# Maxima turned in another bank, first units ahead of the last normed block, and a shorter routing in a six-layer decoder

## The chip, the cores and the metric

The kernel runs on one core of a Trainium2 chip. The metric is device time in microseconds (us) of one execution. The engines named are PE (TensorE, matrix products and transposes), DVE (VectorE), ACT (ScalarE), POOL (GpSimd), and SP (SyncE, which here only issues DMAs). They run side by side, each its own queue in order, and meet at semaphores.

## The reference

Sixteen sequences of 128 tokens with 256 features go through six residual blocks. `_layernorm` is a plain normalisation; each block adds its result to `x`:

```
x = x + _L0_attn_ref(_layernorm(x), ...)      # causal bucket attention, LN, MLP with GELU (256 -> 1024 -> 256)
x = x + _L0_xattn_ref(_layernorm(x), ctx, ...)  # cross attention, rotary with decay
x = x + _L0_ffn_ref(_layernorm(x), ...)       # RMS norm, attention, then a routed MLP:
    topw, topi = top_k(softmax(h2 @ router_w), 2); topw = softmax(topw)      # 8 experts of 512
    moe_out = swiglu(h2, shared) + sum over the 2 experts of topw * swiglu(h2, expert)
x = x + _L1_attn_ref(_layernorm(x), ...)      # retention: (Q K^T * decay) V, group norm
x = x + _L1_xattn_ref(_layernorm(x), ctx, ...)  # cross attention, window of 64, causal
x = x + _L1_ffn_ref(_layernorm(x), ...)       # 16 experts of 128 in 4 groups: the 2 best groups,
    # in them the 2 best experts by softmax score + gate_b; weights from the plain softmax; a shared expert
```

## The kernel before

The program names the stages ATT0, MLP, XATT0, ATT1, MOE0, RET, XATT1 and MOE1. A tile (`Tile`: layer `l`, number `t`) is one sequence of 128 tokens; `x_all` holds all sixteen in on-chip memory. Five hand-written programs, one for each engine, give the order; every hand-over is a semaphore that counts up, `wait(eng, name, tile)`.

`pipeline(eng, layers, step)` runs the attention layers. A step holds several tiles at different ages: `at[3]` is normalised (`variance`, POOL's `inverse_root`, `normalise`, PE's transpose at L979), `at[2]` rotated, `at[1]` gets its values and maxima, `at[0]` its scores and probabilities, `at[-1]` its output product L1044 and the residual addition L1864, and `normed(at)`, which is `at[-2]` where a feed-forward layer follows, is normalised for that layer (L1893, L1895), transposed by PE (`turn_normed`, L1088) and copied and split by ACT and POOL into `fT_hi` and `fT_lo`. In the same late steps POOL splits the coming layer's first weights in pieces (`first_low`, L850).

The row maxima go this way: DVE reduces the scores (L1734), works them in several small operations into `nmx` (L1749 to L1762), PE transposes it (`turn_maxima`, L1052) into PSUM bank `B_V`, which also holds the values and at times the output product, and DVE spreads it into `inj` (`inject`, L1777), which PE adds to the scores by a product.

The dense feed-forward parts (`feed_forward`, MLP and the shared expert of MOE0) take four groups of four tiles (`GT` = 4, `GROUPS` = 4). `up` (L1159) makes, for each unit `fc` of 128 hidden features, 6 matmuls of 512 columns for MLP and 12 for MOE0 (gate and up), as each operand is split in a high and a low part and three products are made. The two units' banks alternate: unit `fc` waits for `act_done` of unit `fc - 2`. `down` (L1159 too) gives `down_out`, `add` (L2198) sums into `x_all` and gives `acc_done`.

The routed parts gather rows. DVE finds each token's two experts (`gate_moe0`, `gate_moe1`), `place` makes running counts over the sixteen tiles by four additions of shifted copies (L2022), PE's `ranks` turn them into ranks, and `slots(f, k)`, k = 0 to 5, make each token's slot; two tables of ones and zeroes (`slot_tile`, `slot_row`, L2071 and L2030) and PE's `origins` (L1221) give for every slot its row (`from_u`). Then tiles of 128 slots (39 in MOE0, 47 in MOE1) run one after another: POOL gathers rows (L684), PE transposes (L1277) and multiplies (L1292, L1304) with the tile's own expert weights, which SP loads (`load_tiles`, L567) into 4 buffers of 1.5 MB (MOE0) or 8 of 385 KB. In MOE0 tile 0 has its buffer early; tiles 1 to 3 wait for the last `acc_done`:

```
sp.wait_ge(S["acc_done"], units("acc_done", f, F_EXPERTS[f] - 1, GROUPS - 1, GT))
```

In MOE0 the steps of the routing (`gate_moe0(0 .. 15)`) are laid between the hidden units of the shared expert; number 15 is `slots(MOE0, 5)`, which waits for PE's `origins` (`hot_out`). In MOE1 all lies between the last attention step and the first tile. MOE0's results come back through DRAM into `y_back` and are added to `x_all` by `combine` (L2289, L2290), tile by tile in RET's first steps. `gate_piece(at)` says which piece of MOE1's gating belongs to a step of XATT1.

## Time and profile before

| | |
|---|---|
| median of 3 runs | 1462.07 us (1457.41 to 1466.78) |
| the profiled execution | 1464.77 us, its span 1462.9 us |
| mean granted TensorE clock | 0.953 of full speed |
| PE busy | 1298.5 us, 89% |
| DVE, ACT, POOL busy | 867.4, 571.1, 705.6 us |
| chain that ended last | PE 61%, DVE 14%, DMA 10%, POOL 5% |

The span runs from the first to the last instruction of one execution. Busy shares are means over stages of different kinds; the chain says which engine's work set the end. The granted clock is in parts of the full 2.4 GHz; 0.50 in a stretch is 1.2 GHz. In the rows below, L and a number is the line of the kernel, and the square bracket is the idle time of that engine ahead of the instruction, with what ended it.

### The profile page before, as it was taken

To read this page: it belongs to the slowest core of one execution; us is meant where nothing else is said; L and a number is where in the kernel's file an instruction comes from. 1 tells how busy PE (TensorE), PEld (TensorE's weight loads), DVE (VectorE), ACT (ScalarE), POOL (GpSimd) and SP (SyncE) were. 2 spreads that over 40 slices of the span, in tenths; PEclk is the share of its full clock that TensorE was granted. 3 is DMA by queue.
4 is the path that set the end of the run, shared out by engine and by line. 5 is a ranking of instruction groups with operands and counts; after the bars stand their busy time and mean duration, and the time that the engine had idled before them with its cause. 6 is when DMAs were issued, how large, how long until landed. Compare 5 with 4: busy or idle time off the path is not lost.

```text
span 1462.9 us, 33803 instructions
## 1 busy us (share of the span) xinstructions
PE 1298.5 (89%) x12132; PEld 1045.0 (71%) x12132; DVE 867.4 (59%) x2050; ACT 571.1 (39%) x1272; POOL 705.6 (48%) x949
## 2 busy tenths in 40 slices
PE   5999979988999999979889999959998999818897
PEld 4666647876777777758889999846765777617776
DVE  4888743337888888736512121158875778773346
ACT  2555535523444455643222222214443555413331
POOL 5566632017667466630223333237784556427426
PEclk9999968998999999989999999979999999958999
DMA  6000000020000000000298999630000000028964
GB/s 252 2 2 0 2 1 30 1 86 16 13 15 5 2 16 15 16 16 1 80 338 314 334 325 328 245 137 30 0 16 9 25 28 26 16 92 284 316 189 144
DMA packets 47370, 137.79 MB, mean 94 GB/s; under 512 B 6925, under 2 KB 29646, under 8 KB 41104
## 3 DMA queue, kind: packets, MB, share of 16 engines
q1 hardware_dynamic: 32944, 110.37, 21.4%
q0 software_dynamic: 7536, 19.67, 4.4%
q10 hardware_dynamic: 6768, 6.16, 1.2%
q8 instruction: 70, 1.15, 0.3%
q14 instruction: 52, 0.43, 0.1%
HBM read 119.54 MB, written 17.56 MB: 94 GB/s over the span
## 4 chain that ended last, share of the span: by engine, by line
PE 61%; DVE 14%; DMA 10%; issue 8%; POOL 5%; ACT 1%; DVEq 0%; SPq 0%; POOLq 0%; ACTq 0%
PE ps L1159 11%; PE ps L1018 8%; PE ps L967 7%; PE ps L1292 7%; PE ps L1066 5%; DMA back_of<-w_odd 4%; DMA row_in<-rows_of,from_u 4%; PE ps L1304 3%; PE ps L1035 3%; PE ps L1044 3%; DVE negmax L1734 3%; PE ps L911 2%; PE ps L958 2%; PE ps L1073 2%; PE ps L993 2%
## 5 line engine op out<-in xcount | busy, mean ns | idle before, releaser
L1292 PE MATMUL ps<-hT,w_tile 128*128 128x128 f32 x1624 | 199.9, 278 | 8.4 <-DMA w_tile<-in_w_f 7.4
L1292 PEld LDWEIGHTS ps<-hT,w_tile 128*128 128x128 f32 x1624 | 190.6, 194 | 12.6 <-issue 7.1
L1358 ACT ACTIVATE probsT_all<-ps 128x1024 f32<-128x1024 f32 x128 | 131.1, 1024 | 158.3 <-PE ps L967 158.3
L1734 DVE TENSOR_REDUCE negmax<-ps 128x8 f32<-128x1024 f32 x128 | 155.9, 1218 | 54.2 <-PE ps L967 53.9
L967 PE MATMUL ps<-qe,kf 32*128 32x256 f32 x1280 | 152.9, 386 | 0.0
L967 PE MATMUL ps<-ke,qf 32*128 32x256 f32 x1024 | 143.6, 398 | 0.0
L747 POOL TENSOR_SCALAR eps_sum<-mv 128x1 f32<-128x1 f32 x112 | 25.4, 227 | 201.0 <-DVE mv L1671 169.4
L967 PEld LDWEIGHTS ps<-qe,kf 32*128 32x128 f32 x1280 | 110.4, 189 | 4.9 <-issue 2.7
L2255 DVE TENSOR_TENSOR h_in<-ps,act_sb 128x512 f32<-128x512 f32 x39 | 27.0, 691 | 143.3 <-PE ps L1292 143.3
L1066 PE MATMUL ps<-probsT_all,va 128*32 128x128 f32 x2560 | 104.4, 281 | 6.1 <-ACT probsT_all L1358 4.4
L691 POOL DMA_INDIRECT back_of<-be,to_u x39 | 39.4, 1010 | 144.7 <-DVE be L2268 144.7
L1304 PE MATMUL ps<-w_tile,h_in 128*128 128x256 f32 x406 | 102.6, 382 | 4.0 <-DVE w_odd L2268 4.0
L1351 ACT ACTIVATE hT<-ps,vecs 128x128 f32<-128x128 f32 x142 | 47.0, 384 | 151.3 <-PE ps L1277 136.8
L1018 PE MATMUL ps<-hT,w_even 128*128 128x128 f32 x640 | 90.3, 288 | 9.2 <-issue 4.7
L1066 PEld LDWEIGHTS ps<-probsT_all,va 128*32 128x32 f32 x2560 | 62.3, 110 | 50.6 <-issue 29.3
L1018 PEld LDWEIGHTS ps<-hT,w_even 128*128 128x128 f32 x640 | 80.6, 198 | 20.3 <-issue 13.3
L967 PEld LDWEIGHTS ps<-ke,qf 32*128 32x128 f32 x1024 | 90.6, 186 | 3.2 <-issue 0.8
L1350 ACT ACTIVATE hT<-ps 128x256 f32<-128x256 f32 x95 | 36.3, 382 | 129.3 <-PE ps L979 61.0
L684 POOL DMA_INDIRECT row_in<-rows_of,from_u x63 | 61.1, 970 | 45.2 <-issue 19.6
L1304 PEld LDWEIGHTS ps<-w_tile,h_in 128*128 128x128 f32 x406 | 70.9, 191 | 11.2 <-issue 4.1
L837 POOL TENSOR_TENSOR fT_lo<-act_sb,fT_hi 128x256 fp32r<-128x256 f32 (+1 forms) x48 | 34.9, 727 | 87.0 <-ACT fT_hi L1350 84.3
L766 POOL TENSOR_TENSOR ke<-kf,const 128x512 f32<-128x512 f32 x64 | 67.2, 1050 | 19.3 <-ACT kf L1351 17.8
(266 smaller groups left out, 3226.8 us busy)
## 6 DMA issues: line engine op xcount, KB each, us to landing
w_tile<-in_w_f SPq DMA_DIRECT2D x39, 1536.0 KB, 9.3
w_tile<-in_w_f SPq DMA_DIRECT2D x47, 385.0 KB, 7.3
back_of<-w_odd ACTq DMA_DIRECT2D x47, 128.0 KB
ctxT<-in_ctxT SPq DMA_DIRECT2D x32, 128.0 KB, 2.1
rows_of<-nv SPq DMA_DIRECT2D x32, 128.0 KB, 1.7
w_even<-in_w_att SPq DMA_DIRECT2D x3, 1024.0 KB, 7.2
y_back<-back_of SPq DMA_DIRECT2D x6, 512.0 KB, 5.0
x_all<-in_x SPq DMA_DIRECT2D x4, 512.0 KB, 10.6
```

Of the source, the lines that this page charges most:

```text
L684: nc.gpsimd.indirect_dma_start(row_at(b), None, rows_dram[f], bass.IndirectOffsetOnAxis(ap=from_u[:, j:j + 1], axis=0)).then_inc(S["row_in ...
L766: return nc.gpsimd.tensor_tensor(dst, src.unsqueeze(2).to_broadcast([P, KC, 2, P]), parity.unsqueeze(1).unsqueeze(3).to_broadcast([P, KC, ...
L967: done[name, half] = mm(ps[:, bank, c * D:(c + 1) * D], a[strip(j), c], b[strip(j), c].rearrange("p i k -> p (i k)"), start=first, stop=fi ...
L1018: last = mm(ps[:, B_QK, m * P:(m + 1) * P], w[:, c, m * P:(m + 1) * P], src[:, c, :], start=(c == 0), stop=(c == KC - 1))
L1035: last = mm(ps[:, B_V, 0:D], src[:, c, :], w[:, c, 2 * D:3 * D], start=(c == 0), stop=(c == KC - 1))
L1066: last = mm(ps[VW * (h % HB):VW * (h % HB + 1), B_O, h // HB * P:(h // HB + 1) * P], va[:, tile.p, h, :], probsT_all[:, (j * HB + n) * P:( ...
L1159: ins = mm(out, a, b, start=first and k == 0, stop=last and k == 2)
L1292: last = mm(ps[:, 2 * which + at.two, fc * P:(fc + 1) * P], w[:, col:col + P], rowT[:, at.two, c, :], start=c == 0, stop=c == KC - 1)
L1304: last = mm(ps[:, 4 + at.two, 0:D], h_in[:, at.two, fc * P:(fc + 1) * P], w[:, first + fc * D:first + (fc + 1) * D], start=fc == 0, stop=f ...
L1351: return nc.scalar.activation(dst, src, ACT.Identity, scale=1.0 if scale is None else scale, bias=0.0 if bias is None else bias)
L1358: nc.scalar.activation(half_of(probsT_all, half), ps[:, 2:4].rearrange("p b n -> p (b n)"), ACT.Exp, scale=HD ** -0.5).then_inc(S["probs"], 1)
L1734: nc.vector.tensor_reduce(m, ps[:, 0:2].rearrange("p b (h k) -> p (b h) k", h=HB), AX.X, ALU.max, negate=True).then_inc(S["s_max"], 1)
```

## The change

1. `turn_maxima` writes bank 2, `inject` reads it there. It waits for the maxima and for the previous tile's probabilities (the reader of bank 2) in place of the values and the residual.
2. POOL does `first_low` ahead of `norm_low`.
3. PE does the first units of the coming dense layer (`FIRST_UNITS`: MLP 2, MOE0 1) ahead of the last normed block's transposes.
4. XATT0's first norm: DVE's `variance` stands ahead of the last group's additions of MLP, POOL's root ahead of its wait for them.
5. MOE0's step 15 of the routing goes behind the additions of the third group. Tile 1's buffer is `w_back`, the memory of `y_back`; its load waits for the last `h_done`, those of tiles 2 and 3 for the last `down_out`.
6. RET's first tiles (`rooted`): the combination stands behind the norm for tile 0, and tile 2's variance, combination and norm go into the step of tile 1.
7. MOE1's routing: one gating piece moves up a step; `place` goes, PE counts straight from `chosen` (`late_ranks`); `slot_row` is built in 32 comparisons with one column of `part` each (`part` is f32 now); the table is scaled by steps of 128 rows so that one accumulation gives the row (`late_origins`), POOL scales the last 8 of 32 blocks; `slots(MOE1, 5)` is one operation.

```diff
+FIRST_UNITS = {MLP: 2, MOE0: 1, MOE1: 0}
+LATE_BLOCKS = 24
-            return (w_tile0, w_tile1, w_tile2, w_tile3)[b][:, 0:f_cols(f)]
+            return (w_tile0, w_back, w_tile2, w_tile3)[b][:, 0:f_cols(f)]
...
+                    elif j == 1:
+                        sp.wait_ge(S["h_done"], units("h_done", f, F_EXPERTS[f] - 1, GROUPS - 1, D_CHUNKS[f]))
                     else:
-                        sp.wait_ge(S["acc_done"], units("acc_done", f, F_EXPERTS[f] - 1, GROUPS - 1, GT))
+                        sp.wait_ge(S["down_out"], units("down_out", f, F_EXPERTS[f] - 1, GROUPS - 1, GT))
...
+                first_low(at)
                 norm_low(normed(at))
-                first_low(at)
...
             def turn_maxima(tile):
                 wait(pe, "nm_sb", tile)
-                wait(pe, "va_sb", tile)
-                out = tile.back(2)
-                wait(pe, "x_done", tile.back(3) if out is not None and out.l == RET else out)
-                tr(ps[:, B_V, 0:P], nmx[:], ident).then_inc(S["m_out"], 1)
+                wait(pe, "probs", tile.back(1))
+                tr(ps[:, 2, 0:P], nmx[:], ident).then_inc(S["m_out"], 1)
...
+                first_units(normed(at))
                 turn_normed(normed(at), at)
...
+                first = rooted(at)
+                if first and not first_crossed(first[0]):
+                    variance(first[0])
...
+                for tile in first[1:]:
+                    variance(tile)
+                    combine(MOE0, tile.t + 1)
+                    normalise(tile)
...
+            def hot_rows(f, k):
+                if f == MOE1:
+                    for i in range(k * NT, (k + 1) * NT):
+                        last = ts(slot_row[:, i], iota_all[:], part[:, 1, i:i + 1], None, ALU.is_equal)
...
+                if step_ == 4 and f == MOE1:
+                    dve.wait_ge(S["tile_nth"], 2)
+                    for a, b, last in ((0, NT, NT), (NT, LATE_BLOCKS, LATE_BLOCKS - NT)):
+                        table = slot_tile[:, a:b, 0:m]
+                        tt(table, table, steps_of[:, 0:last].unsqueeze(2).to_broadcast([P, last, m]), ALU.mult).then_inc(S["row_hot"], 1)
+                    hot_rows(f, 1)
...
+                    if f == MOE1:
+                        ts(from_u[:, 0:m], ps[:, 0, 0:m], -1.0, 0.0, ALU.add, ALU.max).then_inc(S["from_done"], 1)
+                        return
...
-                        if f == MOE0:
+                        if f == MOE0 and fc + 1 < n or f == MOE0 and g + 1 < GROUPS:
                             gate_moe0(q)
...
+                            if f == MOE0 and g + 1 == GROUPS:
+                                gate_moe0(GROUPS * n - 1)
...
+                if f == MLP:
+                    dve.wait_ge(S["acc_done"], units("acc_done", f, n_e, 0, GT))
+                    variance(tiles_of(XATT0, 0))
                 add(n_e, n_e % 2, GROUPS - 1)
```

**PE, from the last attention step of ATT0 into MLP.** Here is PE's order before; L1044 is the last output product, L1088 a normed block's transposes, L1159 MLP's first products.

```order
L993 MATMUL ps<-const,o 128x128 x2
L1088 MATMUL ps<-const,nv 128x128 x2
L1044 MATMUL ps<-w_even,oT 128x256 x2
L1088 MATMUL ps<-const,nv 128x128 x2
L1159 MATMUL ps<-fT_hi,w_hi 128x512
L1159 MATMUL ps<-fT_lo,w_hi 128x512
L1159 MATMUL ps<-fT_hi,w_lo 128x512
L1159 MATMUL ps<-fT_hi,w_hi 128x512
L1159 MATMUL ps<-fT_lo,w_hi 128x512
```

And in the changed kernel, where L1056, L1098 and L1114 are the same three:

```order
L1056 MATMUL ps<-w_even,oT 128x256 x2
L1114 MATMUL ps<-fT_hi,w_hi 128x512
L1114 MATMUL ps<-fT_lo,w_hi 128x512
L1114 MATMUL ps<-fT_hi,w_lo 128x512
L1114 MATMUL ps<-fT_hi,w_hi 128x512
```

(the next eight rows are L1114 too, then)

```order
L1098 MATMUL ps<-const,nv 128x128 x2
L1114 MATMUL ps<-fT_hi,w_hi 128x512
L1114 MATMUL ps<-fT_lo,w_hi 128x512
L1114 MATMUL ps<-fT_hi,w_lo 128x512
L1114 MATMUL ps<-fT_hi,w_hi 128x512
```

Two units, twelve products in all, now stand between the last output product and the last normed block.

**DVE, end of MOE0's shared expert.** Before; L2085 to L2094 are the eight operations of the routing's last step, L2198 the additions, L2255 the first tile's.

```order
L2185 TENSOR_TENSOR hid_lo<-h_tmp,hid_hi 128x512
L2085 COPY scratch<-ps 128x39
L2086 TENSOR_SCALAR scratch<-ps 128x39
L2087 TENSOR_TENSOR scratch<-scratch,ps 128x39
L2088 SCALAR_TENSOR_TENSOR scratch<-scratch 128x39
L2089 TENSOR_SCALAR from_u<-scratch 128x39
L2091 TENSOR_SCALAR scratch<-scratch 128x39
L2092 SCALAR_TENSOR_TENSOR scratch<-ps,scratch 128x39
L2094 SCALAR_TENSOR_TENSOR to_u<-scratch 128x39
L2198 TENSOR_TENSOR x_all<-ps,x_all 128x256 x8
L2255 TENSOR_TENSOR h_in<-ps,act_sb 128x512 x2
```

And in the changed kernel, L2181 to L2189 and L2293:

```order
L2280 TENSOR_TENSOR hid_lo<-h_tmp,hid_hi 128x512
L2293 TENSOR_TENSOR x_all<-ps,x_all 128x256 x4
L2181 COPY scratch<-ps 128x39
L2182 TENSOR_SCALAR scratch<-ps 128x39
L2183 TENSOR_TENSOR scratch<-scratch,ps 128x39
L2184 SCALAR_TENSOR_TENSOR scratch<-scratch 128x39
L2185 TENSOR_SCALAR from_u<-scratch 128x39
L2186 TENSOR_SCALAR scratch<-scratch 128x39
L2187 SCALAR_TENSOR_TENSOR scratch<-ps,scratch 128x39
L2189 SCALAR_TENSOR_TENSOR to_u<-scratch 128x39
L2293 TENSOR_TENSOR x_all<-ps,x_all 128x256 x4
L2354 TENSOR_TENSOR h_in<-ps,act_sb 128x512 x2
```

The routing's eight operations moved from ahead of eight additions to between two groups of four.

**DVE, the second half of MOE1's routing.** Before, from the casts of the slots on (L2062):

```order
L2062 CAST part<-part_u 128x64
L2065 TENSOR_SCALAR scratch<-ends,nth 47x16
L2066 TENSOR_REDUCE expert_f<-scratch 47x1
L2067 TENSOR_SCALAR expert_of<-expert_f 47x1
L2071 TENSOR_TENSOR slot_tile<-iota_all,part 128x1504
L2030 TENSOR_TENSOR slot_row<-iota_all,part 128x2048 x2
L2078 TENSOR_TENSOR slot_tile<-slot_tile,iota_all 128x752
L2085 COPY scratch<-ps 128x47
L2086 TENSOR_SCALAR scratch<-ps 128x47
L2087 TENSOR_TENSOR scratch<-scratch,ps 128x47
L2088 SCALAR_TENSOR_TENSOR scratch<-scratch 128x47
L2089 TENSOR_SCALAR from_u<-scratch 128x47
```

And in the changed kernel:

```order
L2149 CAST part<-part_u 128x64
L2152 TENSOR_SCALAR scratch<-ends,nth 47x16
L2153 TENSOR_REDUCE expert_f<-scratch 47x1
L2154 TENSOR_SCALAR expert_of<-expert_f 47x1
L2158 TENSOR_TENSOR slot_tile<-iota_all,part 128x1504
L2103 TENSOR_SCALAR slot_row<-iota_all,part 128x128 x16
L2165 TENSOR_TENSOR slot_tile<-slot_tile,steps_of 128x752
L2165 TENSOR_TENSOR slot_tile<-slot_tile,steps_of 128x376
L2103 TENSOR_SCALAR slot_row<-iota_all,part 128x128 x16
L2176 TENSOR_SCALAR from_u<-ps 128x47
```

Two wide comparisons are 32 narrow ones, one table operation is two, and five operations at the end are one.

## Rows read from the trace of the kernel before

**Rows 1.** Page, part 4: chain of work that ended last, share of the span by engine
```profile
PE 61%; DVE 14%; DMA 10%; issue 8%; POOL 5%; ACT 1%; DVEq 0%; SPq 0%; POOLq 0%; ACTq 0%
```

**Rows 2.** Timeline, XATT0: start us, us, engine, line, op, out<-in, count, [idle before <-releaser]
```profile
396.36 0.41 DVE L1864 TENSOR_TENSOR x_all<-ps,x_all 128x256 f32 x1
...
396.91 0.30 PE L1052 MATMUL ps<-const,nmx 128*128 128x128 f32 x1 [0.29 <-DVE x_all L1864]
```

**Rows 3.** Waits: who waits <- for what: us, waits, longest
```profile
PE ps L1052 <- DVE x_all L1864: 5.1, 13, 1.1
```

**Rows 4.** Timeline, a steady step of ATT0, DVE
```profile
129.90 0.18 DVE L1671 BATCH_NORM_AGGREGATE mv<-stats 128x2 f32<-128x6 f32 x1
130.01 0.69 DVE L1777 TENSOR_TENSOR inj<-ps,const 128x512 bf16<-128x512 f32 x1
```

**Rows 5.** Timeline, a late step of ATT0, where the first weights are split
```profile
183.52 0.17 DVE L1749 TENSOR_SCALAR nmx<-negmax 128x16 uint32<-128x16 uint32 x1
...
184.32 1.27 POOL L850 TENSOR_TENSOR w_lo<-w_first,w_hi 128x514 fp32r<-128x514 f32 x1
...
184.43 1.19 DVE L1749 TENSOR_SCALAR nmx<-nmx 128x16 uint32<-128x16 uint32 x1
...
186.31 0.30 PE L1052 MATMUL ps<-const,nmx 128*128 128x128 f32 x1 [2.48 <-DVE r_all L1864]
```

**Rows 6.** Windows: us, PE PEld DVE ACT POOL busy, PEclk, DMA, GB/s
```profile
188.00:192.00 4.00, 4.00 (x27) 2.80 (x24) 2.08 (x4) 1.26 (x2) 1.53 (x3) 0.50 0.00 0
```

**Rows 7.** Timeline, end of ATT0 and start of MLP
```profile
222.60 0.69 PE L1088 MATMUL ps<-const,nv 128*128 128x128 f32 x2 [2.88 <-DVE nv L1895]
...
226.00 0.67 ACT L1569 ACTIVATE h_tmp<-ps,f_bias 128x512 f32<-128x512 f32 x1
...
228.20 0.46 PE L1159 MATMUL ps<-fT_hi,w_hi 128*128 128x512 f32 x1
```

**Rows 8.** Timeline, first step of XATT0
```profile
318.19 0.66 PE L979 MATMUL ps<-const,u 128*128 128x128 f32 x2 [3.10 <-DVE u L1700]
```

**Rows 9.** Timeline, last normed block ahead of MOE0
```profile
646.75 0.69 PE L1088 MATMUL ps<-const,nv 128*128 128x128 f32 x2 [2.33 <-DVE nv L1893]
```

**Rows 10.** Timeline, end of MOE0's shared expert and its first tiles
```profile
719.26 0.36 PE L1159 MATMUL ps<-w_hi,hid_hi 128*128 128x256 f32 x1 [2.18 <-DVE x_all L2198]
...
727.91 2.56 SPq L567 DMA_DIRECT2D w_tile<-in_w_f  x3
...
734.83 2.39 PE L1292 MATMUL ps<-hT,w_tile 128*128 128x128 f32 x19 [2.30 <-DMA w_tile<-in_w_f]
```

**Rows 11.** Timeline, RET's first steps
```profile
976.37 0.69 PE L979 MATMUL ps<-const,u 128*128 128x128 f32 x2 [3.15 <-DVE u L1700]
```

**Rows 12.** Timeline, routing of MOE1
```profile
1282.99 0.38 DVE L2008 TENSOR_TENSOR hot<-const,idx_f 128x16 f32<-128x16 f32 x2
...
1284.51 0.41 DVE L1999 MAX8 top<-sc 128x8 f32<-128x16 f32 x4
...
1294.67 0.22 DVE L2156 TENSOR_TENSOR chosen<-hot,sc 128x64 bf16<-128x64 f32 x1
...
1297.46 0.42 DVE L2044 TENSOR_TENSOR scratch<-n_all,steps_of 128x256 f32<-128x256 f32 x1
...
1299.21 0.42 DVE L2052 SCALAR_TENSOR_TENSOR scratch<-ends,scratch 128x256 f32<-128x256 f32 x1
...
1304.28 4.48 DVE L2030 TENSOR_TENSOR slot_row<-iota_all,part 128x2048 bf16<-128x2048 bf16 x2
...
1308.68 0.93 DVE L2078 TENSOR_TENSOR slot_tile<-slot_tile,iota_all 128x752 bf16<-128x752 bf16 x1
...
1310.97 1.46 PE L1221 MATMUL ps<-slot_tile,slot_row 128*128 128x47 bf16 x32 [0.52 <-POOL slot_tile L698]
...
1313.43 0.19 DVE L2089 TENSOR_SCALAR from_u<-scratch 128x47 uint32<-128x47 f32 x1
```

**Rows 13.** Groups by line and form, a tensor_scalar: busy us, mean ns
```profile
L1893 DVE TENSOR_SCALAR nv<-r_all,rstd 128x256 f32 x8 | 2.8, 348 | 0.0
```

More of the change, by code:

```diff
@@ L1027, in project_values @@
                 wait(pe, "va_sb", last)
-                if last is not None and last.l != RET and tile.l != RET:
-                    wait(pe, "inj_sb", last)
                 if tile.l == RET and isinstance(tile.t, int) and tile.t == 0:
@@ L1896, in norm_rows, with rooted @@
                 ins.then_inc(S["n_norm"], 1)
+            def rooted(at):
+                if 3 not in at or at[3].l == RET and at[3].t == 2:
+                    return []
+                tile = at[3]
+                return [tile, tiles_of(RET, 2)] if tile.l == RET and tile.t == 1 else [tile]
             def combine_next(at):
```

185 lines of the change are left out of this document (120 added, 65 removed).

## The prediction, made before the changed kernel ran

> **What bounds the kernel now.** I read the page first: the chain that ended last lies on TensorE (PE) for 61% of the span, on VectorE (DVE) for 14% and on DMA for 10% [rows 1]. An edit therefore pays only where PE stands still, or where the joints between layers run through DVE, ScalarE (ACT) and GpSimd (POOL) one after another. So I took the list of waits for the instructions that the diff touches, then the timeline around each, and asked of every wait which of its inputs came last.
>
> The own time of the profiled execution is 1464.8 us (span 1462.9 and about 2 around it); the three runs shown have a median of 1462.1, so it stands 2.7 above that median. The sum is made against 1464.8. About 1% (14.7 us) is what a measurement of this kernel can tell from no change.
>
> **1. Maxima into bank 2: 4.0.** Before, the transpose of the maxima (L1052) writes the bank of the values and so waits for the residual addition L1864 that reads it; after, it writes bank 2 and needs only `nmx` and the previous tile's probabilities, which PE has used already. At 396 us `nmx` is done by about 396.4, the addition starts 396.36, and PE goes on at 396.91 after 0.29 idle that the addition ended [rows 2]. All such waits for `x_all` come to 5.1 us in 13 cases [rows 3]; where `nmx` itself is as late, nothing comes back, so I take 4.0 (bounds 3 and 5.1). For ATT0 the steady steps give nothing: the injection L1777 that the transpose feeds stands behind an aggregate on DVE's own queue, 129.90 and then 130.01 [rows 4].
>
> **2. POOL's order at the tails: 2.2, and 2.9 for the clock.** Before, the split of the coming layer's first weights (`first_low`, L850) runs after `norm_low` and falls beside DVE's L1749: that bitwise operation starts 0.11 after POOL's 1.27 and takes 1.19, where another of it takes 0.17, and PE's next transpose has stood still for 2.48 [rows 5]. In each of the two last full steps of ATT0 about 1.0 comes back, and about 0.35 by part 1, as there the transpose also waited for `r_all`: 2.7. At ATT1 the same exchange puts a 768-column piece (about 1.27 x 768/514 = 1.9 us) ahead of the norm's work: it may now hold DVE's L1749 for up to 2 (I take 1.5), while in the drain the norm's root no longer stands behind it (about 1.0). Net 2.7 - 1.5 + 1.0 = 2.2. The clock: behind the 2.48 pause the granted clock fell to 0.50 (1.2 GHz) for all of 188 to 192 [rows 6]; that alone costs 2.0, and with the ends of the stretch I estimate 2.9. With a pause of 1.2 instead I let it stay up (upper bound 2.9, lower 0).
>
> **3. Two units of MLP ahead of the last normed block: -2.0.** Before, PE idles 2.88 until 222.60, turns the last block and then works at half speed, 0.63 a matmul, until 228.20 [rows 7]. The two units' 12 matmuls are those of that stretch, 5.2 us; put into the pause at the same clock they end some 2 after the block is ready. What PE fills, others lose: ACT copies the transposed block, loads a table and only then does the first Gelu at 226.00 [rows 7], and all of it stands behind the block's transposes, which now come 1.0 to 1.5 later; the two units' results sit waiting, and the third needs the bank that the first Gelu frees: it starts at 227.7 to 228.5, as before, after a pause of some 3.5 that keeps the clock down for another such stretch. I take -2.0 (bounds +0.5 and -3).
>
> **4. First cross norm ahead of the sums: 2.7.** Before, the last MLP addition is followed by statistics, POOL's root, `u`, and PE's transpose at 318.19 after 3.10 idle [rows 8]. Moved ahead of the four last additions, this chain lies under the last down products; what stays is one addition, its semaphore, and DVE's `u`. I put the transpose near 316.2: 2.0. A pause of 1.1 instead of 3.1 may keep the clock: 0.7 more as a mean over that.
>
> **5. One unit of MOE0 ahead of its last norm: 2.5.** PE idles 2.33 until 646.75 [rows 9]; the first unit stands behind that block. One unit goes into that pause and past it; a second unit has the other banks and waits for nobody. The pause is 2.3; the wait for the block's copy, which is filled too, adds something, and the lateness that the unit gives to the block takes some: 2.5, bounds 1.5 and 3.
>
> **6. Tail of MOE0: 5.8.** Three things. `gate_moe0(15)`, which waits for the origin counts, goes behind the additions of the third group, so PE no longer idles 2.18 at 719.26. Tile 1's weights now lie in `y_back`, which is free until the results are fetched back behind the last tile, so their load waits for `h_done` and not for the last sum; it was issued at 727.91 and PE waited 2.30 for it until 734.83 [rows 10]. Tiles 2 and 3 wait for `down_out`. With a load of 6.9 us (727.91 to 734.83) issued ahead of the last down products, well over 7 earlier, tile 1 is no longer late; tile 0 is bounded by its gathered rows. 2.18 + 2.30 + about 1.3 of a clock that falls less: 5.8 (bounds 4 and 7; the loads and the gathers now share the DMA engines, up to 1.5).
>
> **7. RET's joint: 1.2.** PE idles 3.15 at 976.37 for tile 2's `u` [rows 11], because two combinations stand ahead of it on DVE. They move a step earlier, but the shuffle and the rotation of the tile before bound the step nearly as much: 1.2 (0.9 to 5.0, the latter if PE becomes the bound).
>
> **8. Routing of MOE1: 4.7.** It lies wholly on the path: tiles can't start before `from_u`. (a) One piece of the group before the last moves to an earlier step: L2008 at 1282.99 to the maxima at 1284.51 are 1.5 us. (b) Between `chosen` (ends 1294.89) and the position L2052 (1299.21) lay 4.3 us: four scans, PE, two copies, then the ends. Now PE counts straight from `chosen` (0.5), and compare, reduce and four additions remain, 1297.46 to 1299.21, 1.75 [rows 12]: 2.1 saved. (c) From 1304.28 to the end of `from_u` at 1313.62 lie 9.34: two comparisons in 4.48, 0.93 of table, PE's last 32 products in 1.46 and five small operations. After: 16 small comparisons, table 0.93 + 0.5, 16 again, 32 products, one operation [rows 12]. The price of one 128x128 `tensor_scalar` isn't in the trace. Below: 0.10, one of the four maxima that take 0.41 together at 1284.51. Above: 0.348, which L1893 takes for 256 columns [rows 13]. Nearest is an operation of half those columns with overlapping ends, 0.15: then 2.4 + 1.4 + 2.4 + 1.5 + 0.4 = 8.1, 1.2 saved. At 0.10 it is 2.8 saved, at 0.348 5.1 lost. 1.5 + 2.1 + 1.2 = 4.8; 4.7, since POOL's share of the table (376 instead of 752 columns) must end before the last 16 products and may be held up by DVE.
>
> Two comparisons of 2048 columns of bf16 took 4.48 us, 0.9 columns a ns [rows 12]. The Trainium skill ("VectorE: DVE Perf Modes", the table of tiers) gives a `tensor_tensor` in bf16 twice that rate (1.22 us for 2048), and a `tensor_scalar` in bf16 four times; the trace disagrees on the first, where an operand is broadcast. By its second figure, 128 columns would be 0.03 plus what is fixed, and part 8 an estimated 1.6 more than I take. Its section "The TRN2 errata — SBUF-src ops pay a fixed extra latency per instruction" speaks against cutting one operation into 16; by it the split gives nothing or loses; no row here has such small comparisons.
>
> **Sum.** 4.0 + 2.2 + 2.9 - 2.0 + 2.7 + 2.5 + 5.8 + 1.2 + 4.7 = 24.0. 1464.8 - 24.0 = 1440.8; the same off the median would be 1438.1. I say 1440.
>
> **Rivals.**
> (A) Half is swallowed: what PE gains ahead of a stage is given back inside it, since the tile stages follow their weight loads, the clock falls anyway at two of the three places (-4.6 for parts 2 and 4), and part 6 gives only the 2.18. Then 24.0 - 4.6 - 3.6 - 1.5 = 14.3: 1450. For it speaks that part 3 loses by this very mechanism, against it that the pauses [rows 5, 8, 10] have named releasers that the diff removes.
> (B) The ceiling: all upper bounds of 2, 6 and 7, and 0.10 in part 8: 24 + 1.2 + 3.8 + 1.6 + 2.5 (part 3 neutral) = 33, so 1432.
> (C) The change doesn't do what it says at the joints, because a new wait takes the old one's place in each of parts 3 to 7 (the injection, the rotation, the gather are all within 1 us of what is removed): only parts 1 and 8 and 2.0 remain, 11: 1454.
> (D) Slower: the 32 small comparisons. At 0.348 part 8 gives 3.65 - 5.1 = -1.4 alone. For the whole to be slower than before they must cost 24 us more than forecast, 0.9 each, about what an operation costs when DVE and POOL hold each other back as in [rows 5]: there L1749 took 1.0 more than usual. POOL's table lies beside only some of them, so this needs a price that nothing here shows. From 0.45 each on the gain is under 1%. Time at 1.0 each: 1440.8 + 32 x 0.85 = 1468.
>
> **How the numbers follow.** The forecast 0.50 (1434 to 1446), A 0.22, B 0.10, C 0.14, D 0.04. Each term errs on its own by 1 to 3 us and the runs shown differ by 9, which gives every case a width of about 5 to either side. The range 1427 to 1455 holds most of the first four: below it half of B's tail, above it half of C and D. The bound of faster by over 1% is 1447.4: the forecast nearly whole, B, and 0.3 of A and a little of C: 0.73. Slower by over 1% needs 1476.7: 0.02. The rest, 0.25, is within 1%.
>
> **What would show it.** Right: PE's transpose of the maxima without a wait for `x_all`; L1749 at 0.2 to 0.4 in ATT0's tail and a granted clock near 1.0 behind it; PE's pause ahead of the first cross norm near 1; no wait of tile 1 for its weights; `from_u` ending 8 after the first row comparison begins and the small comparisons near 0.15 each. Wrong: comparisons over 0.25 each, the clock down at the same places, the third unit of MLP well before 227 (then part 3 is a gain), or tiles of MOE0 slowed by gathers. My estimate rests most on part 6 and on the clock of part 2.

## The result, and the profile of the changed kernel

| | before | changed |
|---|---|---|
| median of 3 runs | 1462.07 (1457.41 to 1466.78) | 1446.43 (1442.32 to 1447.47) |
| ratio | | 0.9868 (0.983 to 0.9907) |
| profiled execution | 1464.77, span 1462.9 | 1447.47, span 1445.6 |
| mean granted clock | 0.953 | 0.961 |

The change is faster by 1.3%. The chain that ended last, part 4 of its page, now lies on PE for more of the span, and on DVE, DMA and POOL for less [rows 1]:

```profile
PE 70%; DVE 12%; DMA 8%; issue 5%; POOL 3%; ACT 2%; DVEq 0%; SPq 0%; POOLq 0%; ACTq 0%
```

Where the time went is read best from marks that both programs have: the starts of PE's transposes of the maxima (64 of them), the DVE operations on the hidden units, on the routing and on the tiles. Each cell is the length from the mark before, in us; every mark is the start of its instruction, and the last one is the last residual addition, 2.7 before the end of the span:

| from the mark before to | before | changed | won | forecast (part) |
|---|---|---|---|---|
| ATT0, 2nd maxima (from the start) | 39.01 | 44.18 | -5.17 | |
| ATT0, 13th maxima | 123.57 | 123.26 | 0.31 | 0 (1) |
| MLP, 9th hidden unit | 82.63 | 77.31 | 5.32 | 2.7 + 2.9 (2), -2.0 (3) |
| MLP, last hidden unit | 60.11 | 60.38 | -0.27 | 0 |
| XATT0, 1st maxima | 34.72 | 31.02 | 3.70 | 2.7 (4) |
| XATT0, 15th | 133.75 | 130.44 | 3.31 | 4.0 (1) |
| ATT1, 13th | 129.56 | 129.69 | -0.13 | 0 |
| ATT1, 16th | 26.02 | 26.93 | -0.91 | -1.5 (2) |
| MOE0, 9th hidden unit | 56.04 | 57.06 | -1.02 | 1.0 (2), 2.5 (5) |
| MOE0, last hidden unit | 27.35 | 27.35 | 0 | 0 |
| 2nd tile's `h_in` | 25.95 | 19.54 | 6.41 | 5.8 (6) |
| last tile's | 212.11 | 211.40 | 0.71 | 0 |
| XATT1, 1st maxima | 159.51 | 159.20 | 0.31 | 1.2 (7) |
| XATT1, 16th | 156.81 | 156.57 | 0.24 | 0 |
| MOE1, last `chosen` | 27.53 | 25.25 | 2.28 | 1.5 (8a) |
| `slot_row` | 9.61 | 7.40 | 2.21 | 2.1 (8b) |
| last operation of the routing, `from_u` | 9.15 | 8.74 | 0.41 | 1.2 (8c) |
| tiles and residual additions, to the last addition | 146.80 | 147.09 | -0.29 | 0 |

All that lies behind the start won 22.5 together. The start took 5.2 longer in this execution; that is no doing of the change, as the first run below shows. Each column is one execution, and some of the stages below differ by more than the change between executions of the same instructions.

The rows that answer to those shown of before are these. The timeline of XATT0, beside [rows 2]: the transpose starts 0.17 after the addition has begun and waits for nothing; of the waits of [rows 3] none is left.

```profile
392.18 0.41 DVE L1921 TENSOR_TENSOR x_all<-ps,x_all 128x256 f32 x1
...
392.35 0.29 PE L1062 MATMUL ps<-const,nmx 128*128 128x128 f32 x1
```

The end of ATT0, beside [rows 5]: POOL's split now lies ahead of the bitwise operation L1806, which takes 0.17, and PE's pause is 1.04 instead of 2.48. The two windows (columns as in [rows 6]) show the clock at full speed, the first one there, the second behind the joint of MLP and XATT0.

```profile
185.67 1.27 POOL L862 TENSOR_TENSOR w_lo<-w_first,w_hi 128x514 fp32r<-128x514 f32 x1
...
189.41 0.17 DVE L1806 TENSOR_SCALAR nmx<-nmx 128x16 uint32<-128x16 uint32 x1
...
189.85 0.33 PE L1062 MATMUL ps<-const,nmx 128*128 128x128 f32 x1 [1.04 <-DVE negmax L1816]
```

```profile
188.00:192.00 4.00, 2.04 (x30) 1.16 (x29) 3.59 (x13) 1.75 (x5) 1.41 (x3) 1.00 0.00 0
318.00:322.00 4.00, 2.71 (x24) 2.47 (x24) 0.92 (x3) 1.42 (x5) 0.61 (x1) 1.00 0.95 338
```

Into MLP, beside [rows 7]. Times in the two traces are best counted from the start of the last output product, which is the first row here for the kernel before and the second for the changed one:

```profile
217.64 2.07 PE L1044 MATMUL ps<-w_even,oT 128*128 128x256 f32 x4
```

```profile
216.66 2.07 PE L1056 MATMUL ps<-w_even,oT 128*128 128x256 f32 x4
...
218.17 0.99 PE L1114 MATMUL ps<-fT_hi,w_hi 128*128 128x512 f32 x1
...
220.54 0.40 PE L1114 MATMUL ps<-fT_hi,w_lo 128*128 128x512 f32 x1
...
221.15 0.41 DVE L1952 TENSOR_SCALAR nv<-r_all,mv,rstd 128x256 f32<-128x256 f32 x1 [1.05 <-POOL rstd L826]
...
221.94 0.40 PE L1114 MATMUL ps<-fT_hi,w_lo 128*128 128x512 f32 x1
...
222.18 0.38 PE L1098 MATMUL ps<-const,nv 128*128 128x128 f32 x2
...
225.28 0.67 ACT L1626 ACTIVATE h_tmp<-ps,f_bias 128x512 f32<-128x512 f32 x1
...
226.09 0.47 PE L1114 MATMUL ps<-fT_hi,w_hi 128*128 128x512 f32 x1 [3.53 <-ACT h_tmp L1626]
```

The early products begin at 218.17 and are at full speed by 220.54; the last of the twelve starts at 221.94. The last block, ready at 221.56, is turned at 222.18: 5.5 behind the output product, where it was 5.0 before. The third unit waits 3.53 for the first Gelu and starts 9.4 behind the output product, where it was 10.6.

Then XATT0's first transpose, beside [rows 8]: a pause of 1.17 for 3.10.

```profile
316.27 0.41 PE L993 MATMUL ps<-const,u 128*128 128x128 f32 x2 [1.17 <-DVE u L1757]
```

MOE0's first tiles, beside [rows 10]: tile 1's products (weights in `y_back`) follow tile 0's without a pause.

```profile
718.22 0.44 PE L1334 MATMUL ps<-const,row_in 128*128 128x128 f32 x2 [0.52 <-DVE x_all L2293]
...
719.52 3.81 PE L1349 MATMUL ps<-hT,w_tile 128*128 128x128 f32 x32 [0.17 <-ACT hT L1408]
...
723.39 3.74 PE L1349 MATMUL ps<-hT,y_back 128*128 128x128 f32 x32
```

RET's first steps, beside [rows 11], on PE and DVE: new pauses of 2.50 and 1.89 stand in place of the 3.15.

```profile
963.26 2.69 PE L1032 MATMUL ps<-hT,w_odd 128*128 128x128 f32 x16 [2.50 <-ACT hT L1407]
...
969.56 2.34 DVE L1784 TENSOR_TENSOR probsT_all<-ps,const 128x1024 f32<-128x1024 f32 x2
...
970.92 0.75 PE L1076 MATMUL ps<-probsT_all,va 128*32 128x128 f32 x16 [1.89 <-DVE probsT_all L1784]
```

MOE1's routing, beside [rows 12]; in brackets again the idle time ahead and what ended it:

```profile
1279.58 0.22 DVE L2251 TENSOR_TENSOR chosen<-hot,sc 128x64 bf16<-128x64 f32 x1
...
1281.93 0.42 DVE L2134 SCALAR_TENSOR_TENSOR scratch<-ends,ps 128x256 f32<-128x256 f32 x1
...
1286.98 3.27 DVE L2103 TENSOR_SCALAR slot_row<-iota_all,part 128x128 bf16<-128x128 bf16 x16
...
1288.72 0.83 POOL L710 TENSOR_TENSOR slot_tile<-slot_tile,steps_of 128x376 bf16<-128x376 bf16 x1 [14.64 <-ACT tile_in L1408]
...
1295.72 0.21 DVE L2176 TENSOR_SCALAR from_u<-ps 128x47 uint32<-128x47 f32 x1 [1.55 <-PE ps L1252]
...
1296.79 1.16 POOL L693 DMA_INDIRECT row_in<-rows_of,from_u  x1 [7.24 <-DVE from_u L2176]
...
1300.29 0.69 PE L1334 MATMUL ps<-const,row_in 128*128 128x128 f32 x2 [4.60 <-DMA row_in<-rows_of,from_u]
```

### The profile page after: what moved, and what is told of

Read it like the earlier page. It is cut to its first block, busy times and chain, and to the rows that moved or that the text cites. A ratio compares the mean times of both kernels' runs of the same rounds, so it can differ in the third digit from the quotient of the medians.

```text
span 1445.6 us, 33878 instructions
## 1 busy us (share of the span) xinstructions
PE 1301.3 (90%) x12165; PEld 1048.3 (73%) x12165; DVE 863.6 (60%) x2071; ACT 571.2 (40%) x1272; POOL 702.4 (49%) x949
## 4 chain that ended last, share of the span: by engine, by line
PE 70%; DVE 12%; DMA 8%; issue 5%; POOL 3%; ACT 2%; DVEq 0%; SPq 0%; POOLq 0%; ACTq 0%
PE ps L1114 11%; PE ps L981 9%; PE ps L1032 9%; PE ps L1349 8%; PE ps L1076 6%; PE ps L1056 4%; PE ps L1047 4%; PE ps L1361 4%; DMA row_in<-rows_of,from_u 4%; DMA back_of<-w_odd 3%; PE ps L925 2%; PE ps L972 2%; DVE negmax L1791 2%; PE ps L1083 2%; PE ps L1007 2%
## 5 line engine op out<-in xcount | busy, mean ns | idle before, releaser
L1349 PE MATMUL ps<-hT,w_tile 128*128 128x128 f32 x1304 | 161.9, 278 | 0.6 <-ACT act_sb L1673 0.2
L1349 PEld LDWEIGHTS ps<-hT,w_tile 128*128 128x128 f32 x1304 | 153.3, 193 | 3.1 <-issue 0.8
L1076 PEld LDWEIGHTS ps<-probsT_all,va 128*32 128x32 f32 x2560 | 62.8, 110 | 51.8 <-issue 30.4
L1032 PEld LDWEIGHTS ps<-hT,w_even 128*128 128x128 f32 x640 | 83.0, 203 | 20.4 <-issue 13.2
L1361 PE MATMUL ps<-w_tile,h_in 128*128 128x256 f32 x326 | 83.8, 383 | 9.5 <-DVE w_odd L2367 9.4
L2280 DVE TENSOR_TENSOR hid_lo<-h_tmp,hid_hi 128x512 fp32r<-128x512 f32 x56 | 38.8, 693 | 54.8 <-ACT hid_hi L1407 54.8
```

The costliest lines, as they stand in the source:

```text
L1032: last = mm(ps[:, B_QK, m * P:(m + 1) * P], w[:, c, m * P:(m + 1) * P], src[:, c, :], start=(c == 0), stop=(c == KC - 1))
L1076: last = mm(ps[VW * (h % HB):VW * (h % HB + 1), B_O, h // HB * P:(h // HB + 1) * P], va[:, tile.p, h, :], probsT_all[:, (j * HB + n) * P:( ...
L1349: last = mm(ps[:, 2 * which + at.two, fc * P:(fc + 1) * P], w[:, col:col + P], rowT[:, at.two, c, :], start=c == 0, stop=c == KC - 1)
L1361: last = mm(ps[:, 4 + at.two, 0:D], h_in[:, at.two, fc * P:(fc + 1) * P], w[:, first + fc * D:first + (fc + 1) * D], start=fc == 0, stop=f ...
```

## The experiments

Each run changes one thing in the changed kernel, where nothing else is said. In two of the four groups of runs every kernel takes longer in the last stage (64 us for 51), and the kernel before is slower there by as much (medians of 1482 and 1484 for 1464 and 1465), so times are compared as ratios to the kernel before on the same chip, or as stages between the marks above.

**The changed kernel once more.** No edit.

> The changed kernel itself once more, to see what repeats. Theory A (the stages of the first trace are the change's doing): the start up to the third tile's transposes, the half-speed stretches of TensorE at the end of ATT0 (from about 202), at the end of ATT1 (from about 627) and the stage lengths repeat within 0.5 us; ratio 0.983 to 0.991. Theory B (the 4.7 us longer start, and the clock that fell at 627 instead of 641, are chance of one execution): at least one of them differs in this trace, by 2 us or more.

Median 1465.11, before 1482.22; ratio 0.9864 (0.9836 to 0.9892). The start up to the second maxima took 39.11, not 44.18, and 38.3 to 39.9 in each of the eleven other runs below: the 5.2 are chance. Less this shift the clock fell where it had in the first trace (at 198 and 621, there at 203 and 627), and the stages up to MOE0's tiles repeat within 0.5. Behind them two do not: MOE0's tiles took 2.1 more, and the way to the last `chosen` 30.27 instead of 25.25. So theory B holds for the start and for these two, and theory A for the stages between, as far as two executions tell.

MOE0's tiles, from the second to the last, took from 205.6 to 214.5 us in all the fourteen traces, and the edits below don't order them. The clock is not the reason, being at full speed almost throughout; PE waits for gathered rows. Here are these waits in the shortest (`first_low` first at ATT0 only, 205.6) and in the repeated changed kernel (213.5), as us in total, times, longest:

```profile
PE ps L1338 <- DMA row_in<-rows_of,from_u: 1.0, 1, 1.0
```

```profile
PE ps L1334 <- DMA row_in<-rows_of,from_u: 7.3, 9, 1.6
```

What makes the gathers late in one execution and not in another stays open.

**POOL's order.**

```diff
-                first_low(at)
                 norm_low(normed(at))
+                first_low(at)
```

> The changed kernel with one edit undone: POOL does norm_low ahead of first_low again. Theory A (the order of POOL brought the gain at the end of ATT0 and cost something at the end of ATT1): at the end of ATT0 DVE's L1806 beside the split takes 1.2 again instead of 0.2, the pause of PE is about 2.1 (2.5 less the 0.35 of the bank), the clock falls near 186 to 190, and 3 to 5 us are lost there; at the end of ATT1 0.5 to 0.9 come back and the clock falls near 641 and not near 627, 2.5 more; total +0 to +2 us. Theory B (the bank alone keeps the clock up at ATT0's end): the clock stays up to 200 there, only 1 to 2 us are lost, and the total is 1 to 2 us faster than the changed kernel.

Ratio 0.9831 (0.9806 to 0.9857). DVE's L1806 was blocked again, with PE's pause at 2.06:

```profile
184.54 1.27 POOL L862 TENSOR_TENSOR w_lo<-w_first,w_hi 128x514 fp32r<-128x514 f32 x1
...
184.65 1.19 DVE L1806 TENSOR_SCALAR nmx<-nmx 128x16 uint32<-128x16 uint32 x1
...
186.10 0.33 PE L1062 MATMUL ps<-const,nmx 128*128 128x128 f32 x1 [2.06 <-DVE negmax L1816]
```

From the 13th maxima of ATT0 to MLP's ninth hidden unit 80.87: 3.6 of the 5.3 won there are lost without the order (1.02 in the first of the two steps, the rest in the second and in the clock, which fell near 188 again). At the end of ATT1 1.06 came back (9.32 and 8.11 for 9.84 and 8.65). Theory A, but for the clock at ATT1's end: it fell at 625, not near 641. The time of the whole doesn't show the 3.6: the median is 1459.03 against 1465.11 of the changed kernel on the same chip, lower and not higher, with intervals of the ratios that overlap.

**The order at ATT0's end alone.** `first_low` first only where `normed(at)` is ATT0's.

> The changed kernel, but first_low ahead of norm_low only where MLP follows (end of ATT0); ahead of MOE0 norm_low comes first again. Theory A (at ATT1's end the early split delays DVE and POOL, PE gets more pauses and its clock falls 14 us earlier): the step at 606 loses nothing (0.6 to 0.9 back) and the clock stays up until about 640: 2.5 more, so 3 to 3.5 us faster than the changed kernel. Theory B (the earlier fall of the clock is chance or comes from elsewhere): only 0.6 to 0.9 us back and the clock falls near 627 all the same.

Ratio 0.9827 (0.9801 to 0.9853). The 1.06 came back. From ATT1's last maxima to MOE0's ninth hidden unit it took 53.02 instead of 57.03, the clock being down only from 630 to 633. By itself this speaks for theory A; the next paragraph shows that it doesn't settle it.

**What the clock does by itself.** The same stretch, from ATT1's last maxima to MOE0's ninth hidden unit, in the eight executions that have the changed kernel's instructions up to there: six from 56.98 to 57.52, but also 52.30 and 50.70. The length goes with the time for which the clock was down between the two marks: 17 us in the six, 3.4 us in the one of 52.30, none in the one of 50.70. With POOL's other order it is 56.04 (before) and 55.91 with 13.7 us, 53.02 and 52.97 with 3.4 us. At the end of XATT1 the way to the last `chosen` took 25.1 to 25.3 in eight of the thirteen traces of the changed kernel and its variants, 26.4 in three and 30.3 to 30.4 in two, with edits that don't touch it. Two executions, both with the same instructions up to here, in windows of 4 us (columns as in [rows 6]); first the repeated changed kernel, where the clock falls in the first window and stays down, then the run called `gate_moe0` back below, where it doesn't fall at all:

```profile
618.00:622.00 4.00, 2.31 (x17) 1.48 (x17) 2.22 (x6) 2.30 (x4) 2.35 (x5) 0.88 0.10 33
622.00:626.00 4.00, 3.99 (x29) 2.37 (x29) 0.00 (x0) 0.77 (x3) 0.96 (x1) 0.50 0.00 0
```

```profile
618.00:622.00 4.00, 2.46 (x24) 1.68 (x28) 2.02 (x6) 2.24 (x4) 2.47 (x4) 1.00 0.09 33
622.00:626.00 4.00, 3.99 (x52) 2.81 (x44) 0.72 (x2) 2.13 (x5) 1.18 (x2) 1.00 0.00 0
```

A fall there costs up to 6.8 us, more than any row of the table above won, and whether it comes is not set by the instructions alone. What sets it stays open. At the same 3.4 us the stretch took 52.30 with `first_low` first and 53.0 without, while the two steps ahead of it took 1.06 more with it: together a loss of 0.4 at ATT1's end, once the clock is left out.

**MOE1's row comparisons wide.**

```diff
-                if f == MOE1:
-                    for i in range(k * NT, (k + 1) * NT):
-                        last = ts(slot_row[:, i], iota_all[:], part[:, 1, i:i + 1], None, ALU.is_equal)
-                    last.then_inc(S["row_hot"], 1)
-                    return
```

> The changed kernel with the 32 narrow comparisons of hot_rows in MOE1 as two wide ones of 2048 columns again (the rest of the new routing kept). In the changed kernel 16 narrow ones took 3.27 and 2.68 us, a wide one takes 2.28. Theory A (the split is a loss, the rule that small tiles pay per instruction holds): from the start of slot_row to the end of from_u 8.95 becomes 7.5 to 8.0, 1.0 to 1.4 us faster. Theory B (the wide ones hold up POOL's part of the table as before, when its 752 columns took 4.9 us and ended with DVE's last): POOL's 376 columns take over 2 us, PE's last 16 products wait for them, and it is within 0.5 us of the changed kernel.

Ratio 0.9835 (0.9804 to 0.9867). From `slot_row` to `from_u` 7.38 instead of 8.74, so the split into 32 is a loss of 1.36, although beside the wide ones POOL took 4.73 for its 376 columns (0.83 in the changed kernel). Theory A. But the first tile came 9.22 after `from_u` instead of 7.9 to 8.2: of the 1.36 only 0.2 to 0.3 was left. The timeline: the gather is issued at 1292.36, PE gets its rows at 1297.16, 4.80 later (3.50 in the changed kernel); eight loads of weights went out from 1283.10 on.

```profile
1283.10 8.15 SPq L576 DMA_DIRECT2D w_tile<-in_w_f  x8
...
1285.64 4.73 POOL L710 TENSOR_TENSOR slot_tile<-slot_tile,steps_of 128x376 bf16<-128x376 bf16 x1 [14.63 <-ACT tile_in L1408]
...
1292.36 1.15 POOL L693 DMA_INDIRECT row_in<-rows_of,from_u  x1 [1.99 <-DVE from_u L2171]
...
1297.16 1.11 PE L1334 MATMUL ps<-const,row_in 128*128 128x128 f32 x4 [5.91 <-DMA row_in<-rows_of,from_u]
```

The DMA engines' busy share between issue and use of the rows (the last column but one) is 0.50 in the changed kernel, the first of these windows, and 0.70 here, the second (columns as in [rows 6]):

```profile
1296.79:1300.29 3.50, 0.01 (x1) 0.01 (x1) 0.84 (x5) 0.00 (x0) 2.89 (x3) 0.50 0.50 170
```

```profile
1292.36:1297.16 4.80, 0.00 (x1) 0.00 (x1) 0.83 (x5) 0.00 (x0) 3.88 (x4) 0.50 0.70 243
```

**The loads let go with the gather.** The wide comparisons, and

```diff
+                        if f == MOE1 and j == 4:
+                            sp.wait_ge(S["from_done"], 2)
```

> The changed kernel with MOE1's row comparisons wide again and, new, the loads of expert weights from the fifth tile on waiting until from_u is there. With wide comparisons alone from_u came 1.36 us sooner, but the first gathered rows landed 4.8 us after their issue instead of 3.5, and the first tile no sooner. Theory A (the gather shares the DMA engines with eight loads of 385 KB that fill them until 12.5 us after the row comparisons began): with four loads ahead instead of eight the rows land 3.5 after the issue, from_u to the first tile is 8.1 again, 1.0 us won there; the tiles behind may lose up to 4 us for the loads that come later. Theory B (the landing is late for another reason): from_u to the first tile stays at 9.2.

Ratio 0.9854 (0.9816 to 0.9891). `from_u` to the first tile 11.36: neither theory's number. The loads were let go in the moment in which the gather was, stood ahead of it and met it; the landing took 5.36, at a DMA share of 0.79:

```profile
1290.77 1.16 POOL L695 DMA_INDIRECT row_in<-rows_of,from_u  x1 [1.99 <-DVE from_u L2173]
...
1296.13 0.69 PE L1336 MATMUL ps<-const,row_in 128*128 128x128 f32 x2 [6.47 <-DMA row_in<-rows_of,from_u]
```

**The loads behind the first rows.** The same with `sp.wait_ge(S["row_out"], tiles_before(f, 1))`.

> As the run with the deferred loads, but the loads from the fifth tile on wait until PE has turned the first gathered rows (there they were let go together with the gather, and met it again). Theory A (contention with the weight loads is what makes the first rows late): the rows land 3.5 us or less after the issue of their gather, from_u to the first tile is 8.2 or less instead of 9.2 (all loads ahead) and 11.4 (loads let go with the gather); slot_row to the first tile 15.6, 1.2 less than the changed kernel's 16.8. The tiles behind take up to 5 us longer for the late loads. Theory B (lateness from elsewhere): from_u to the first tile 9 or more.

Ratio 0.9837 (0.9789 to 0.9885). The landing took 3.56, at a DMA share of 0.23, `from_u` to the first tile 8.07, `slot_row` to the first tile 15.45 instead of 16.8, and the tiles behind 91.96, in the midst of the six executions that are as slow in the last stage and have all loads ahead (90.8 to 94.7). Theory A: what the first gather waits for is the traffic of the weight loads. With all loads ahead the changed kernel escapes this, since its longer routing issues the gather 1.4 later.

```profile
1291.31 1.16 POOL L695 DMA_INDIRECT row_in<-rows_of,from_u  x1 [1.98 <-DVE from_u L2173]
...
1294.87 0.69 PE L1336 MATMUL ps<-const,row_in 128*128 128x128 f32 x2 [4.67 <-DMA row_in<-rows_of,from_u]
```

**No early units.** `FIRST_UNITS = {MLP: 0, MOE0: 0, MOE1: 0}`.

> The changed kernel with no units ahead of the last normed block, neither for MLP nor for MOE0. Theory A (the prediction's: at MLP the units cost 2.0, at MOE0 they give 2.5): from the last maxima of ATT0 to MLP's ninth hidden unit 2 us shorter, from the last maxima of ATT1 to MOE0's ninth hidden unit 2.5 longer. Theory B (the traces': at MLP the two units end before the block is ready, so they cost nothing and give nothing but the clock's state; at MOE0 they give about 2): within 0.7 at MLP, 2 longer at MOE0, each blurred by up to 2 to 3 us where a half-speed stretch of TensorE falls elsewhere.

From the last maxima of ATT0 to MLP's ninth unit 44.21 (44.17 to 44.64 with units, in the five executions where the step before was the same 10.29); from ATT1's last to MOE0's ninth 57.21, where 56.98 to 57.52 stand with the unit and as long a time at the low clock. Nothing at MLP, as theory B has it; about nothing at MOE0, where both theories have 2 or more. At MOE0, without the unit the last block is turned at 636.75 and the first silu starts at 642.01; with it (the repeated run, whose marks lie 0.76 later) the block is turned at 639.83, the silu starts at 644.17, and the third unit, whose bank it frees, waits for it:

```profile
636.75 0.66 PE L1098 MATMUL ps<-const,nv 128*128 128x128 f32 x2 [2.49 <-issue]
...
642.01 0.60 ACT L1629 ACTIVATE act_sb<-ps 128x512 f32<-128x512 f32 x1
```

```profile
639.83 0.38 PE L1098 MATMUL ps<-const,nv 128*128 128x128 f32 x2
...
644.17 0.58 ACT L1629 ACTIVATE act_sb<-ps 128x512 f32<-128x512 f32 x1
...
644.81 0.50 PE L1114 MATMUL ps<-fT_hi,w_hi 128*128 128x512 f32 x1 [0.38 <-ACT act_sb L1629]
```

Less the 0.76 the block is turned 2.3 later with the unit. Only 1.3 of these are the twelve products': the last output product, which they follow, starts at 631.67 and 633.43, so 1.0 had been lost ahead of them: the clock stayed down there in the run with the unit and was up from 628 to 632 in the one without. Behind the block come ACT's copy, the router's softmax, the table load and the first silu. Counted from the output product the silu starts 0.4 later with the unit, and the ninth hidden unit 1.2 sooner (41.3 for 42.5), with the clock down for 4.6 us of that way and not 10.2. So this pair bounds what the unit gives at 1.2; how much of it is the clock, one execution can't tell. At MLP it is the same: without units the clock was down for 24 us from the 13th maxima to the ninth unit, with them for 17 to 21.

**The maxima in the values' bank.** `turn_maxima`, `inject` and `project_values` as before.

> The changed kernel with the maxima turned in the values' bank again, with the waits of before. Theory A (the residual addition is what the bank saves, 0.2 to 0.3 in each of XATT0's steps): from XATT0's first to its fifteenth maxima 133.5 to 133.9 instead of 130.4 us, ATT1 and XATT1 and the steady steps of ATT0 unchanged within 0.1. Theory B (XATT0's gain came with the clock at the joint instead): that stretch stays at 130.4.

XATT0 134.47 instead of 130.44. That is 0.6 beyond theory A's range, which was taken from the trace of before; the step from the first to the second maxima took 0.8 more than there, the clock being down in more of it. From the second to the fifteenth maxima undoing the bank costs 4.1. Theory A, and the wait is back in the timeline:

```profile
393.65 0.30 PE L1066 MATMUL ps<-const,nmx 128*128 128x128 f32 x1 [0.28 <-DVE x_all L1925]
```

Two things are not as expected. The steady steps of ATT0 took 0.4 more, where nothing was forecast. And from ATT0's 13th maxima to MLP's ninth hidden unit it took 82.53, as long as before: of the 5.3 won there 5.2 went, although POOL's order was kept and the bitwise operation took 0.17. In the first of the two steps that is 0.3, in the second 2.9, with the clock down from 186 to 193, and 2.0 in MLP's start, with the clock down again. The order undone costs 3.6 and the bank undone 5.2, so the two are not parts of a sum: the gain there hangs on the clock's course, and what the bank does to it one execution doesn't show.

**RET's order as before.** `rooted` returns `[at[3]]`.

> The changed kernel with RET's first tiles in the order of before (tile 2's variance, combination and norm in their own step, the combination ahead of tile 0's norm). Theory A (the moved norm gives 3.1 us at RET's third step, which the next step gives back, since DVE's rotation and next norm and the clock bound it): from the last tile of MOE0 to XATT1's first maxima within 0.5 us of the changed kernel's 159.2 to 159.4. Theory B (the prediction's 1.2, what the move saves stays saved): 160.4 or more.

The pause of 3.15 for `u` is back, and the stage takes 158.95, within theory A's 0.5. But the executions that have the new order take from 157.38 to 159.39 (160.43 in the one with the bank back), with different courses of the clock, a spread wider than the 1.2 that is asked about. The one whose clock is down in two stretches as long as here, 10 and 7 us, took 158.16 (tile 1's buffer back): PE reached tile 2's transpose 3.75 sooner after MOE0's last tile, paused for 3.27 instead of 0.47 right behind it, reached the next tile's transpose 0.8 sooner, and kept the 0.8. So most of what the moved norm wins is given back in the next step; whether 0.8 or nothing stays, the runs don't settle.

```profile
955.28 0.69 PE L991 MATMUL ps<-const,u 128*128 128x128 f32 x2 [3.15 <-DVE u L1755]
```

**`gate_moe0` back.** The routing's last step ahead of all additions.

> The changed kernel with only the place of MOE0's last routing step undone (gate_moe0(15) ahead of both groups of additions). Theory A (the two edits at MOE0's tail each remove their own wait): PE idles 2.2 again before its last down products, from the last hidden unit to the first tile 18 to 19.6 us instead of 15.8, from the first to the second tile 3.7 as in the changed kernel. Theory B (the buffer and the earlier loads do it all): 15.8 to 16.3. Elsewhere as the changed kernel but for where the clock falls.

Last hidden unit to first tile 19.68 (15.81), first to second 3.74. Theory A; of the 3.9 PE's pause is 2.19, and the clock, down from 703 to 706, has the rest, as before:

```profile
702.04 0.36 PE L1114 MATMUL ps<-w_hi,hid_hi 128*128 128x256 f32 x1 [2.19 <-DVE x_all L2293]
```

**Tile 1's buffer and the loads' waits back.**

> The changed kernel with tile 1's weights in their old buffer and the loads of tiles 1 to 3 waiting for the last sum again. Theory A: the first tile as early as in the changed kernel (15.8 us after the last hidden unit), the second 6.0 to 7.0 after the first instead of 3.7, so 2.3 to 3.3 lost. Theory B (the early loads delay the gathers): the first tile 0.5 to 1.5 earlier than in the changed kernel, and the loss smaller by that.

First tile as early (15.80), the second 8.17 behind it (3.73): 4.4 lost, 1.1 more than the expectation's upper end. PE's wait for the load is 2.54, near the 2.30 of before; the surplus is the clock, which fell behind the wait (723.4 to 726.8), so that the tile's first 32 products took 5.46 instead of 3.74. The first tile was not earlier by any of theory B's 0.5.

```profile
715.70 3.29 SPq L574 DMA_DIRECT2D w_tile<-in_w_f  x3
...
722.87 5.46 PE L1347 MATMUL ps<-hT,w_tile 128*128 128x128 f32 x32 [2.54 <-DMA w_tile<-in_w_f]
```

**The parts that held, together.** `first_low` first at ATT0's end only, wide comparisons, loads behind the first rows.

> The changed kernel with what the runs have shown to be better put together: first_low ahead of norm_low only where MLP follows, MOE1's row comparisons wide, and the expert weights from the fifth tile on loaded when the first gathered rows have been turned. Theory A (the three hold together): the two steps at the end of ATT1 are 9.3 and 8.1 instead of 9.8 and 8.65 (1.06 won), slot_row to the first tile 15.5 instead of 16.8 (1.4 won), all else as the changed kernel; 2.5 us faster than it, ratio to the kernel before 0.978 to 0.986. Theory B (the clock's falls outweigh it): the stages show these 2.5, but the ratio does not differ from the changed kernel's 0.986 by more than its interval.

Median 1438.77, before 1465.01; ratio 0.9832 (0.9789 to 0.9875). The two steps of ATT1 took 9.32 and 8.11, `slot_row` to the first tile 15.49, the tiles 86.78: 2.4 of the 2.5 us are in the stages. In the ratio they can't be told from the changed kernel's 0.9868 and 0.9864: theory B's reading, its stages being theory A's.

## Why the prediction was right, and where it was not

The time came in the range and on the side that was forecast; by the own time of the execution it was 1447.5 against 1440.8, and 5.2 of these 6.7 are the start, which the sum didn't hold. Behind the start the stages gave 22.5 of the 24.0. That this is so near is in part luck: parts 3, 4, 6 and 8a gave more than forecast and parts 5, 7 and 8c less, and single stages move by 2 to 9 us between executions of the same instructions. Against the median the gain is 15.6: the 22.5 less the start's 5.2 are the 17.3 between the two profiled executions, of which the one of before stood 2.7 over its median and the changed one 1.0 over its own.

**Part 1** (4.0) held: 3.3 in the trace, 4.0 by undoing it. At the steady steps of ATT0, put at nothing, it gave 0.3 to 0.4.

**Part 2** held at ATT0 as a sum with the clock (5.3 against 5.6, and 1.0 for the order in the first step), but not as two terms: the order undone lost 3.6 and the bank undone 5.2. That the clock stays up was a wager. The second step took 10.29 in six of the twelve executions with this order, 11.7 to 11.8 in five with the clock down for 3.4 us near 187, and 13.2 in the one with the bank back. At ATT1 the step "I take 1.5" measured 1.06, so it was over-sized.

**Part 3** (-2.0) measured 0 from mark to mark. The step that failed is "put into the pause at the same clock they end some 2 after the block is ready": they began at 218.17, the clock rose at 220.4 in their midst, and the block was turned 0.6 after it was ready (0.5 to 1.2 in the twelve executions with the units). The third unit did wait for the Gelu (3.53), but it didn't start "as before": counted from the last output product it came 1.1 sooner, and in this execution the clock, down again from 227 to 231, took that back.

**Part 4** (2.7) measured 3.7 here and in seven other executions: behind the pause of 1.17 the clock here stayed at 1.00 for 10 us, which I had weighed at 0.7. In five others it fell behind the pause, and 2.6 to 2.8 were won. No run undoes this part alone, so its size rests on the comparison with the one trace of before.

**Part 5** (2.5) measured 0.2 by undoing it, and 1.2 at most counted from the last output product; the 1.02 that the table shows lost there is the clock, down from 627 and for 17 us instead of from 641 and for 14. The step that failed is "the lateness that the unit gives to the block takes some": the unit turned the block 1.3 later, and with the clock's course beside it nothing of the 1.5 to 3 is seen. How the two share in it stays open.

**Part 6** (5.8) measured 6.4, 3.9 for the routing's last step and up to 4.4 for the buffer and the loads; the two overlap in part, as both of these hold a fall of the clock of 3.4 us.

**Part 7** (1.2) measured 0.3; undoing it leaves anything from nothing to 0.8.

**Part 8** (4.7) measured 4.9, by two errors: (a) gave 2.3 for 1.5, (c) 0.4 for 1.2. Of these (a) is not sure: no run undoes it, and its stage took 1.1 less than before in three executions and 2.8 more in two. The term that was mis-sized in (c) is the small comparison at 0.15: the sixteen took 3.27 beside POOL's table and 2.68 without, 0.20 and 0.17 each, against 2.28 for a wide one. The section of the Trainium skill that spoke against the split ("VectorE: DVE Perf Modes", "The TRN2 errata — SBUF-src ops pay a fixed extra latency per instruction") gives a fixed extra price for each instruction, and the trace agrees with it: 16 small ones cost 0.4 to 1.0 more than one large.

Of the rivals, A's time (1450) lay nearer to the median than the forecast, by 3.6 against 6.4; its mechanism, gains given back in the next stage, is seen in part 7 and perhaps in part 5. D did not come: a comparison cost 0.20 at most, as a mean of sixteen.

## What to carry to other kernels

Work put into a pause of one engine ahead of a transfer to the next one delays that transfer: follow the delayed hand-over (block, copy, table, activation, bank) to its end before the pause is counted as won. When a setup chain gets shorter, look what else is in flight where it ends: here the first gather met eight weight loads, and only with them held back did the shorter routing reach the tiles. And compare stages between marks, over several executions, when the clock's falls are larger than the edits; put beside each length how long the clock was down in it, as two executions that differ there say nothing of the edit.

## What the runs showed of the hardware

With identical instructions up to that point, TensorE's granted clock stayed at 1.00 (2.4 GHz) through the end of ATT1 in one execution and went to 0.50 (1.2 GHz) for 17 us in another; PE was busy for 2.46 and 2.31 us of the 4 us in which they part. The stretch behind took 50.7 and 57.0 us. A POOL multiplication of 376 columns took 0.83 us beside DVE's narrow `tensor_scalar` operations and 4.73 beside its wide `tensor_tensor`. An indirect gather of rows landed 3.5 us after its issue with the DMA engines busy for a share of 0.23 or 0.50 meanwhile, 4.8 at 0.70 and 5.4 at 0.79.
